# The partly filled third of the rows comes second, with shared gate and up products, its last 21 rows made directly, and the next tile's y earlier

## The reference

```
y   = einsum('bct,bcd->bdt', x, cond_weights[itok])       # 2048 rows of 1024
gate, up = oct_ternary_linear(y, w_gate), oct_ternary_linear(y, w_up)   # 8 x 342 outputs each
h   = silu(gate) * up
out = x + oct_ternary_linear(h, w_down)                   # back to 1024

def ternary_dequant(W): scale = mean(abs(W)); return scale * clip(round(W / scale), -1, 1)
def oct_ternary_linear(xp, W):                            # S_OCT: signs of the octonion product
    M = einsum('jik,jod->koid', S_OCT, ternary_dequant(W)); return einsum('...id,koid->...ko', xp, M)
```

## Time and profile before

| | us |
|---|---|
| median of 3 runs | 723.91 |
| lowest, highest | 722.75, 724.21 |
| the profiled execution | 724.41 |
| its span, first to last instruction | 722.6 |
| TensorE busy in the span | 687.3 |
| VectorE busy | 538.6 |
| ScalarE busy | 332.3 |
| GpSimd busy | 352.5 |

### The profile page before, as it was taken

The page is one execution under the profiler, slowest core; times in us unless marked ns, Lnnn a source line. Parts: engine busy times, 40 slices in busy tenths (PEclk is TensorE's granted clock), DMA queues, the critical chain, the costliest instruction groups (busy, mean ns, idle before and its releaser), DMA issues.

```text
span 722.6 us, 17130 instructions
## 1 busy us (share of the span) xinstructions
PE 687.3 (95%) x7046; PEld 625.0 (86%) x7046; DVE 538.6 (75%) x867; ACT 332.3 (46%) x530; POOL 352.5 (49%) x409
## 2 busy tenths in 40 slices
PE   3679998999999999999999999999999999999995
PEld 3468887999999989999899999999899998988895
DVE  1898956767876688676877678766877678777877
ACT  5543485155444546255452555344452554434531
POOL 0200557435736466344856356364753357464553
PEclk9799999999999999999999999999999999999999
DMA  8100003021002110031001110031000300021001
GB/s 327 59 2 1 1 2 122 30 89 64 1 2 88 33 61 2 2 118 63 1 2 52 66 63 2 2 117 62 4 1 11 108 2 1 2 88 31 1 2 59
DMA packets 10576, 31.51 MB, mean 44 GB/s; under 512 B 3330, under 2 KB 3330, under 8 KB 10370
## 3 DMA queue, kind: packets, MB, share of 16 engines
q1 hardware_dynamic: 9906, 28.81, 11.2%
q10 hardware_dynamic: 592, 1.61, 0.7%
HBM read 22.02 MB, written 8.39 MB: 42 GB/s over the span
## 4 chain that ended last, share of the span: by engine, by line
PE 85%; DVE 7%; ACT 3%; issue 2%; POOL 1%; DMA 1%; ACTq 0%; DVEq 0%; POOLq 0%
PE ps L1016 58%; PE ps L1108 21%; PE ps L1003 4%; DMA cond_bd<-in_L_cond_weights_dram 1%; DVE pu_sb L723 1%; ACT down_c L705 1%; POOL z_f L531 1%; PE ps L1010 1%; DVE o_sb L443 1%; ACT z_op L632 1%; DVE ps L843 1%; POOL h_pairs L531 1%; DVE z_op L830 0%; ACT ps L652 0%; DVE gate_table L723 0%
## 5 line engine op out<-in xcount | busy, mean ns | idle before, releaser
L1016 PE MATMUL ps<-y_op,gate_table 128*128 128x256 f16 x2112 | 273.0, 275 | 5.7 <-DVE y_op L816 4.2
L1016 PE MATMUL ps<-y_op,up_table 128*128 128x256 f16 x2112 | 270.7, 273 | 0.2 <-DVE up_table L768 0.2
L1016 PEld LDWEIGHTS ps<-y_op,gate_table 128*128 128x128 f16 x2112 | 207.6, 99 | 30.6 <-DVE y_op L816 4.3
L1016 PEld LDWEIGHTS ps<-y_op,up_table 128*128 128x128 f16 x2112 | 207.1, 98 | 25.1 <-DVE up_table L768 0.7
L531 POOL TENSOR_TENSOR h_pairs<-h_f 128x256 f32<-128x256 f32 (+1 forms) x128 | 121.1, 975 | 151.8 <-ACT h_f L618 94.1
L531 POOL TENSOR_TENSOR z_f<-h_pairs 128x512 f32<-128x512 f32 x80 | 102.7, 1305 | 102.6 <-DVE z_op L830 100.8
L652 ACT ACTIVATE ps<-ps,small 128x512 f32<-128x512 f32 x96 | 63.6, 662 | 175.5 <-DVE ps L843 125.4
L443 POOL TENSOR_TENSOR o_sb<-o_sb,wd_sb 128x256 f32<-128x256 f32 (+1 forms) x150 | 88.3, 626 | 92.7 <-DVE wd_sb L891 91.5
L1108 PE MATMUL ps<-down_c,h_op 128*128 128x128 f16 x1536 | 93.1, 220 | 3.0 <-ACT down_c L705 3.0
L723 DVE TENSOR_TENSOR pu_sb<-ps,q_sb 128x512 f32<-128x512 f32 x96 | 65.8, 686 | 38.7 <-ACT q_sb L646 26.0
L1108 PEld LDWEIGHTS ps<-down_c,h_op 128*128 128x128 f16 x1536 | 89.8, 98 | 4.0 <-ACT down_c L705 3.1
(11 more groups left out here) (75 smaller groups left out, 480.7 us busy)
## 6 DMA issues: line engine op xcount, KB each, us to landing
x_in<-in_x_dram SPq DMA_DIRECT2D x8, 1024.0 KB, 5.3
o_sb<-in_x_dram SPq DMA_DIRECT2D x16, 512.0 KB, 3.6
out_dram<-o_sb SPq DMA_DIRECT2D x15, 512.0 KB, 2.7
h_op<-in_L_ffn_w_gate_dram ACTq DMA_DIRECT2D x3, 512.0 KB, 6.8
h_op<-in_L_ffn_w_up_dram SPq DMA_DIRECT2D x3, 512.0 KB, 7.4
z_op<-in_L_ffn_w_down_dram SPq DMA_DIRECT2D x1, 1536.0 KB, 11.4
out_dram<-o_sb SPq DMA_DIRECT2D x2, 256.0 KB, 2.1
cond_bd<-in_L_cond_weights_dram SPq DMA_DIRECT2D x30, 16.0 KB, 3.0
```

What stands on the lines that cost most here:

```text
L1016: mm = pe.matmul(dst, table[m][:, slot, q, :], y_op[:, op, e, :], start=(i == 0 and e == 0), stop=(i == len(terms) - 1 and e == 1))
```

## The change

The windows are taken in the order 0, 2, 1, so that the partly filled one comes second (`MID = 1`) as chunks 4 to 7. Its rows are split: the first 64 (`HALF`) keep the shared products, the last 21 (padded to 32, `REST`) are made without sharing.

- For the 64 rows, gate and up of a sum stand side by side in one 128-column weight (`mid_table`), so that one matmul gives gate on partitions 0 to 63 and up on 64 to 127. A middle chunk has 16 own and 4 shared matmuls, a pair 4 in common. It uses one bank, `bank_mid` (banks 0, 3, 1, 4).
- ScalarE copies up from partitions 64 to 127 to SBUF (`mid_u`, in the place of `ud_sb`), since the product takes both on the same partitions. The split of h comes behind the chunk's silu, and that of the last chunk behind it too.
- For the other 32 rows, `direct` holds for each of eight parts the plain weights (16 small copies in the first tile), four outputs side by side; `rest(T, i)` makes parts 2i, 2i + 1 and their partners in 32 matmuls, i = 0 in bank 0 and i = 1 in bank 3, behind chunk 7. ScalarE and VectorE treat them with `rest_silu`, `rest_h`, `split_rest` and `rest_lo`.
- z and the down products of this window use 96 partitions.
- y of the next tile is made behind chunks 0 to 3 and the norms behind 5; z 0 and z 1 are taken behind chunks 7 and 8, and the scales stay behind chunk 8.

The core of the diff:

```diff
+    MID, HALF, REST = 1, P // 2, P // 4
+    ROWS = [P, HALF + REST, P]
-    Y_AFTER = {1: 0, 2: 1, 4: 2, 5: 3}
-    NORM_AFTER = 7
+    Y_AFTER = {0: 0, 1: 1, 2: 2, 3: 3}
+    NORM_AFTER = 5
+    SCALES_AFTER = 8
-    Z_LO_AFTER = {6: 0, 7: 1, 10: 2, 11: 3}
+    Z_LO_AFTER = {7: 0, 8: 1, 10: 2, 11: 3}
...
+            def rest_silu(T, i):
+                n = 2 * T + i
+                act.wait_ge(rest_done, n + 1)
+                act.wait_ge(h_ready, NC * T + 4 * MID + 3 + i)
+                act.activation(mid_u(i), bank_rest(i)[HALF:P], ACT.Copy)
+                gate = bank_rest(i)[0:HALF]
+                act.activation(gate, gate, ACT.Silu, scale=gate_scale(T)[0:HALF]).then_inc(rest_silu_ready, 1)
+
+            def split_rest(T, i):
+                act.wait_ge(rest_h_ready, 2 * T + i + 1)
+                slots_of_i = slice(4 * MID + 2 * i, 4 * MID + 2 * i + 2)
+                for h in range(2):
+                    last = act.activation(h_op[HALF:HALF + REST, slots_of_i, h, 0, :],
+                                          bank_rest(i)[REST * h:REST * h + REST], ACT.Copy)
+                last.then_inc(rest_hi_ready, 1)
+                for h in range(2):
+                    last = act.activation(h_f[HALF:HALF + REST, slots_of_i, h, :],
+                                          bank_rest(i)[REST * h:REST * h + REST], ACT.Copy)
+                last.then_inc(rest_copied, 1)
...
-                if c > 0:
+                if c == 4 * (MID + 1):
+                    split_rest(T, 1)
+                elif c > 0 and (w != MID or K == 0):
                     split_h(T, c - 1)
...
+                if w == MID:
+                    if T > 0 and K == 0:
+                        act.wait_ge(wd_ready, SUB * T)
+                    act.wait_ge(h_ready, n - 1)
+                    act.activation(mid_u(K), bank_mid(K)[HALF:P], ACT.Copy).then_inc(u_ready, 1)
+                    gate = bank_mid(K)[0:HALF]
+                    act.activation(gate, gate, ACT.Silu, scale=gate_scale(T)[0:HALF]).then_inc(silu_ready, 1)
+                    if K > 0:
+                        split_h(T, c - 1)
...
+                    if c == 4 * MID + 3:
+                        split_h(T, c)
+                        rest_silu(T, 0)
+                        split_rest(T, 0)
+                        rest_silu(T, 1)
...
+            def mid_chunk(T, c):
...
+                p = p_sb[:, 0]
+                signed_add(p, bank_mid_pr(K), q_sb[:, K // 2], G2[K // 2] if K % 2 else 1).then_inc(p_ready, 1)
+                if K == 0:
+                    h_lo(T, c - 1)
...
+                add_p(bank, bank, 0, K).then_inc(g_ready, 1)
+                if K > 0:
+                    mid_h(T, c - 1)
+                if K > 1:
+                    h_lo(T, c - 2)
...
+                if c == 4 * (MID + 1):
+                    rest_lo(T, 1)
+                elif c > 0:
                     h_lo(T, c - 1)
...
+                    if c == 4 * MID + 3:
+                        mid_h(T, c)
+                        h_lo(T, c - 1)
+                        h_lo(T, c)
+                        rest_h(T, 0)
+                        rest_lo(T, 0)
+                        rest_h(T, 1)
...
+            def rest(T, i):
+                pe.wait_ge(h_lo_ready, NC * T + 4 * MID + i + 1)
+                pe.wait_ge(h_copied, NC * T + 4 * MID + i + 1)
...
+                for k in range(2):
+                    for j in range(8):
+                        for e in range(2):
+                            mm = pe.matmul(bank_rest(i)[:, k], direct_weights(2 * i + k, j), y_op[:, j, e, :],
+                                           start=(j == 0 and e == 0), stop=(j == 7 and e == 1))
...
+                if 0 <= c - 4 * (MID + 1) < 2:
+                    pe.wait_ge(rest_lo_ready, 2 * T + c - 4 * (MID + 1) + 1)
```

More of the change, by code:

```diff
@@ L169, in build @@
     NU = NC // 2
+    MID, HALF, REST = 1, P // 2, P // 4
+    assert NQ == 3 and count // (8 * P) - 2 * P <= HALF + REST
+    ROWS = [P, HALF + REST, P]
     NR = 2 * NQ
@@ L612, in split_h @@
                     act.wait_ge(tern_ready[1], c // 4 + 1)
-                act.activation(h_op[:, c, :, 0, :], bank_r(s, 0), ACT.Copy).then_inc(h_hi_ready, 1)
+                mid = CHUNKS[c][1] == MID
+                rows = slice(0, HALF) if mid else slice(0, P)
+                bank = (bank_mid(CHUNKS[c][0]) if mid else bank_r(s, 0))[rows]
+                act.activation(h_op[rows, c, :, 0, :], bank, ACT.Copy).then_inc(h_hi_ready, 1)
                 if T > 0 and c % 4 == 0:
@@ L768, in build_table @@
                 dve.tensor_scalar(to(11, 3), to(5, 3), -1.0, None, ALU.mult).then_inc(built, 1)
+                if w == MID:
+                    for h in range(2):
+                        for high in range(2):
+                            src = t[:, 4 * (h ^ high):4 * (h ^ high) + 4, HALF:HALF + REST]
+                            signs = [kind[h] for kind in KINDS[high]]
+                            for sign in (1, -1):
+                                kinds = [k for k in range(3) if signs[k] == sign]
+                                step = kinds[-1] - kinds[0] or 1
+                                dst = direct[:, kinds[0]:kinds[-1] + 1:step, 4 * high:4 * high + 4, m, h, :]
+                                dve.tensor_scalar(dst, src.rearrange("p (a j) o -> p a j o", a=1).broadcast_to(
+                                    [P, len(kinds), 4, REST]), float(sign), None, ALU.mult).then_inc(direct_built, 1)
             def scales_of_tile(T):
@@ L935, in _ @@
                         z_lo(T, z_after[c])
[L936 removed]
+                    if T > 0 and T + 1 < NT and c == SCALES_AFTER:
                         scales_of_tile(T + 1)
@@ L1026, in shared_pair @@
                     pe.wait_ge(ud_ready, SUB * (T - 1) + 1)
-                for m in range(2):
-                    mm = group(bank_q[:, m], m, [(slots[wq[K // 2, b]], q, 12 + b) for b in range(2)])
+                for m in [K // 2] if q == MID else range(2):
+                    mm = group(bank_q[:, m], m, q, [(slots[wq[K // 2, b]], 12 + b) for b in range(2)])
                 mm.then_inc(q_done, 1)
@@ L1185, in _ @@
                             row_norms(T + 1)
+                    if c == 4 * MID + 3:
+                        for i in range(2):
+                            rest(T, i)
                 if T + 1 < NT:
```

161 lines of the change are left out of this document (129 added, 32 removed).

## The result

The changed kernel takes 753.7 us in the median (753.2 to 756.0), the kernel before 724.0 beside it (722.8 to 724.2): a ratio of 1.043, 95% interval 1.041 to 1.044. It is slower, as forecast, but by 29.7 us where 13.2 were forecast, and the time lies above the range. The profiled execution took 753.85 us.

What follows compares the result with a forecast made beforehand. TensorE bound the kernel before; ScalarE's longer chain would bind the changed one. First tile +4.7, tiles 1 to 6 +7.6, last tile +0.9 gave +13.2 us on 723.9: 737 us, range 728 to 746, 72 in 100.

Steps and rivals of the forecast that it cites:

- the price of the narrow operations in the chain: ScalarE and VectorE operations on 64 or 32 partitions: taken to cost the same as on 128, as an upper bound.
- four copies "19.04": Rest's first half on ScalarE: its four copies end at 19.04 us after chunk 4's start, VectorE's product at 16.98.
- the walk: Chain through one tile from chunk 4 to down: 40.59 us, waits 3.9 against 2.62 saved, +1.27 a tile.
- TensorE's saving: Chunks 4 to 7 and rest: 24 fewer matmuls, 2.62 us a tile, 21.0 us in eight.
- Places of the waits: TensorE waits at chunk 5, the rest, chunks 8, 9, 10 and down: 0.3, 0.2, 0.76, 0.05, 1.5, 1.06 us.
- ScalarE's load: ScalarE's busy time over the kernel rises from 332 to about 390 us.
- The first tile: Not bound by TensorE; tables and ScalarE's tail make it 4.7 us later, bounds +2 to +8.
- The last tile: No y, norm or scales; waits of 3.2 us and last z 0.36 later: +0.9 us.
- The clock didn't fall: Rival, 1 in 10: TensorE's clock falls after waits, once a tile 1.65 us, giving 747 us.
- Faster because narrow operations are cheap: Rival, 14 in 100: narrow operations cost less; turns at 87% of the price, 706 us at half price.
- y's move at no cost: Next tile's y rounds, made earlier in the tile, move and cost TensorE the same.
- GpSimd not binding: GpSimd in the tile's chain: does not bind, z2 ready by 35.4 us, needed at 36.95.

Runs made afterwards that it cites:

- the first experiment: Changed kernel with all narrow ScalarE and VectorE operations reading and writing from partition 0, down product's middle window over 64 rows: 739.3 us, ratio 1.024.
- the run with the scales in the gap: Changed kernel with next tile's ten scale operations between product and low parts of the rest's first half, instead of behind chunk 8: 748.1 us.
- the run with the early y alone: Kernel before, with only next tile's y moved behind chunks 0 to 3 and its norm behind chunk 5: 728.1 us, ratio 1.007.
- the run with GpSimd held back: Changed kernel with scales between the rest's first product and low parts, and GpSimd's pairs for z 3 waiting for z 2's low part: 753.7 us.
- the run with steps put where an engine waits: Changed kernel with silu to SBUF, rest's copies by row blocks, and scale and z steps moved to where VectorE and ScalarE wait: 729.0 us.

## Why the prediction was right and wrong

**The step that failed** is the price of the narrow operations in the chain ("I take the same"; four copies "19.04", the silu behind the copy of up 0.49 later). The duration was right: 0.58 to 0.59 us on 64 and 32 rows. The start of the next one was not: the forecast took the 0.49 and 0.60 of operations that all begin at row 0, and called that the upper bound. Operations that begin elsewhere start 0.59 to 0.63 apart on ScalarE and 0.69 to 0.73 on VectorE. With the operations put back to row 0, the walk holds (40.77 us against 40.59), so this one term is 42.72 - 40.77 = 1.95 us of the 2.13 missed in each tile. Over the kernel the first experiment gives back 14.4 of the 16.5 us missed, with a loss of its own of 3 in it. A smaller term is z 1's low part: the step behind it starts 1.45 us later (366.87 to 368.32 on VectorE), where the walk had 1.15; GpSimd is at its sums of y then.

By the Trainium skill (VectorE: DVE Perf Modes, Two Vector instructions with no wait between them) a Vector instruction is held until every earlier one has finished when an input starts in another group of 32 partitions than the last instruction's that read the same memory, or its output in another than the last one written there. The trace agrees, down to the add of up at 365.09: its input starts where the add before it read, but its output goes to SBUF at row 0, and the last output to SBUF was the rest's, at row 64. The page says it of VectorE; ScalarE's rows here behave the same. The page gives no price. With the one measured here, the sum would have had about 2 us more in each tile.

**TensorE's saving**: right. 6.0 lost less 2.62 saved gives 3.4 a tile, and 86.71 - 83.29 is 3.42.

**Places of the waits**: right, all six in their order, with L944 and L930 as named. Sizes as lost time, forecast and measured: 0.3 and 0.33 at chunk 5, 0.2 and 0.43 at the rest, 0.76 and 1.47 at chunk 8, 0.05 and 0.77 at 9, 1.5 and 1.97 at 10, 1.06 and 0.99 at down. The two that follow the rest's tail were short by half and more.

**ScalarE's load**: forecast about 390 busy, measured 399.5.

**The first tile**: 6.1 where 4.7 stood, inside its bounds of 2 to 8. The walk had VectorE's tail in it, but not what TensorE does behind a long wait. Chunk 8's own part, in TensorE's timeline of the changed kernel:
```profile
88.58 3.60 PE L1185 MATMUL ps<-y_op,gate_table 128*128 128x256 f16 x16 [3.13 <-DVE h_op L944]
91.97 3.16 PE L1185 MATMUL ps<-y_op,up_table 128*128 128x256 f16 x16
```
Behind 3.13 us of idle time the 32 matmuls take 6.4 us instead of 3.5. TensorE's granted clock from 86 to 98 us is 0.72. With the rows at 0 that wait is 1.42, the 32 matmuls take 3.5, and tile 1 starts 3.9 us earlier (137.67). Where that kernel is 5.2 us ahead, behind these matmuls (89.78 against 94.97), 2.3 stood before them and 2.9 came in them, which is the clock's part. It is not the same in each execution: the run with the scales in the gap changes nothing in the first tile, and there, behind the same wait (3.14), the first 16 matmuls take 3.32 us but the next 16 only 1.91, while tile 1 starts at 142.58. Before, too, one first tile ended at 135.42 and the same instructions, in the run with the early y alone, at 133.63. So the 6.1 us, read from one execution of each kernel, holds to a microsecond or two.

**The last tile**: 2.8 where 0.9 stood, 0.9 in the first experiment (88.33 - 87.46).

**The rivals.** The clock didn't fall in the steady tiles: behind 1.81 us the next 16 matmuls take 1.92, and the mean clock is 0.987. By the Trainium skill (TensorE: Matmul & The Clock Gate, A second HAM failure mode) frequent short idles would make it go up and down; six waits of 0.2 to 1.8 us a tile didn't do that here. Waits of 3.13 and 3.50 us, once each, did bring it down, in the first tile and in the run with GpSimd held back. Faster because narrow operations are cheap: refuted. They are busy as long as full ones, and cost more where they change place. y's move at no cost: right inside this kernel, wrong by itself in the kernel before (+5.1 us, with the scales that follow it). GpSimd not binding: right for the changed kernel; it bound as soon as the others were quicker.

## What to carry to other kernels

Price an engine's operation by when the next may start, not by its duration, and ask of each one in which row its inputs and its output begin: a kernel that saves matmuls by packing things into parts of the 128 rows pays for each change of place on ScalarE and VectorE. Order such operations by place, so that neighbours begin at the same row. When one wait is taken out, look up what is late next, and what falls together with what, before counting on its length: 1.95 us of scales gave 1.13, and only when VectorE's, ScalarE's and GpSimd's steps had all been moved did the saved matmuls show, with 1.1 to 1.4 us a tile of their 2.62.

## What the hardware showed that I had not expected

- ScalarE starts an operation 0.47 to 0.50 us behind a copy of 512 elements if both begin at the same rows, and 0.59 to 0.63 if not. What counts is the change from the operation ahead: copies that read at row 0 and write at row 64 follow each other at 0.50.
- On VectorE the same costs 0.69 to 0.73 instead of 0.60, and a full-width operation two places behind the narrow ones can still be held (0.73 at 365.09).
- In the down product a change of the number of rows to or from 64 cost 0.09 to 0.10 us (1.89 instead of 1.79 for 32 matmuls); between 128 and 96 rows it cost nothing.
- VectorE's low part of z (1024 elements, SBUF to SBUF) took 1.22 to 1.23 us with GpSimd idle, 1.3 to 1.7 beside GpSimd's sums of y, and 2.05 where it began during the last of its pairs. Held apart from the pairs it was 1.22 again. But this is no fixed price: in the run with steps put where an engine waits it fell onto pairs too and took 1.39, while it was GpSimd that slowed, to 3.47 us for two pairs instead of 2.49. Timelines of GpSimd and VectorE there:
```profile
361.09 3.47 POOL L570 TENSOR_TENSOR h_pairs<-h_f 96x512 f32<-96x512 f32 x2 [0.17 <-POOL z_f L570]
```
```profile
362.04 1.39 DVE L947 TENSOR_TENSOR z_op<-z_f,z_op 96x1024 f16<-96x1024 f32 x1 [1.59 <-ACT z_op L693]
```
Both fit that one waits until the other's running operation has ended: the 2.05 us end 1.08 behind the end of the pairs (376.81 against 375.73). That is read from these rows and was not tried by itself.
